# The output projection of the cross attention in three passes of rounded and remaining parts

## What is computed

```
x = x + xattn(layernorm(x), ctx_2048, mask)   # 16 heads of 16 over 257 context rows
x = x + attn(layernorm(x))                    # causal, ternary weights
x = x + ffn(layernorm(x))                     # quantized, 704 wide
```

```
out  = einsum('bhlm,bmhd->blhd', softmax(...), v).reshape(B, L, 256)
out  = out @ wo.T                             # the output projection
gate = sigmoid(rmsnorm(x) @ wg.T)
return gate * out
```

## Time and profile before

| what | us |
|---|---|
| median of 3 runs | 576.29 |
| lowest, highest | 575.0, 815.79 |
| the profiled execution | 573.81 |
| its span (first to last instruction) | 572.0 |

### The profile page before, as it was taken

How to read it: one execution, slowest core, us unless ns; L and a number is a source line. 1 busy time by engine, 2 the same in 40 slices (tenths; PEclk the granted TensorE clock), 3 DMA queues, 4 the chain that set the end, 5 groups by cost and what they waited for, 6 DMA issues and landing times. The chain is left out here.

```text
span 572.0 us, 20510 instructions
## 1 busy us (share of the span) xinstructions
PE 537.9 (94%) x7142; PEld 449.1 (79%) x7142; DVE 445.7 (78%) x1389; ACT 425.1 (74%) x1208; POOL 323.4 (57%) x490
## 2 busy tenths in 40 slices
PE   7898999999999999999999999999999999987785
PEld 6687788788887888888888878888888877865564
DVE  2667585888978787888979787878879776889664
ACT  5987898697878878787977787787878777773221
POOL 5241848566565748566555658475665648372610
PEclk9999999999999999999999999999999999999988
DMA  8532503214233231413142332414142404000000
GB/s 253 182 94 100 144 21 101 58 49 102 59 84 81 71 83 37 126 32 90 54 107 59 77 78 46 117 33 107 39 103 58 105 5 113 21 13 21 24 9 10
DMA packets 42805, 42.34 MB, mean 74 GB/s; under 512 B 16080, under 2 KB 33488, under 8 KB 42704
## 3 DMA queue, kind: packets, MB, share of 16 engines
q1 hardware_dynamic: 42704, 41.03, 27.3%
HBM read 38.26 MB, written 2.75 MB: 72 GB/s over the span
## 5 line engine op out<-in xcount | busy, mean ns | idle before, releaser
L874 ACT ACTIVATE pr<-sm,nb 128x257 f32<-128x257 f32 x256 | 129.2, 508 | 9.4 <-DVE nb L1110 8.0
L662 POOL TENSOR_TENSOR cTl<-cx,cTh 128x516 fp32r<-128x516 f32 x64 | 84.3, 1317 | 75.1 <-ACT cTh L771 75.0
L1110 DVE CUSTOM_DVE_ANT_0 sm<-x_ps,mbias 128x257 f32<-128x257 f32 x256 | 99.3, 419 | 21.9 <-PE x_ps L1416 20.2
L771 ACT ACTIVATE pt<-x_ps 128x512 f32<-128x512 f32 x112 | 65.3, 599 | 10.5 <-PE x_ps L1426 6.9
L1426 PE MATMUL x_ps<-tab,pr 128*128 128x128 f32 x512 | 71.4, 274 | 0.8 <-DVE o L1141 0.4
L771 ACT ACTIVATE kk<-x_ps 128x257 f32<-128x257 f32 x128 | 49.5, 389 | 22.1 <-PE x_ps L1308 22.1
L1426 PEld LDWEIGHTS x_ps<-tab,pr 128*128 128x128 f32 x512 | 57.3, 141 | 5.8 <-issue 4.4
L1308 PE MATMUL x_ps<-cTh,wkTh 128*128 128x258 f32 x256 | 59.7, 315 | 0.4 <-ACT pt L771 0.3
L670 POOL TENSOR_TENSOR sr<-sv,halfneg 128x20 f32<-128x20 f32 x16 | 56.7, 3541 | 1.3
L1308 PE MATMUL x_ps<-wvTh,cTh 128*128 128x256 f32 x256 | 56.8, 303 | 0.0
L1308 PE MATMUL x_ps<-cTl,wkTh 128*128 128x258 f32 x256 | 51.4, 282 | 0.6 <-POOL cTl L662 0.6
(11 more groups left out here) (193 smaller groups left out, 1342.7 us busy)
## 6 DMA issues: line engine op xcount, KB each, us to landing
cx<-in_ctx SPq DMA_DIRECT2D x64, 258.0 KB, 3.9
mbias<-mask_bias SPq DMA_DIRECT2D x64, 128.5 KB, 3.4
xq<-in_x SPq DMA_DIRECT2D x16, 128.0 KB, 2.9
xr<-in_x SPq DMA_DIRECT2D x16, 128.0 KB, 2.8
vx<-end_values SPq DMA_DIRECT2D x64, 32.0 KB, 2.3
vr<-self_values SPq DMA_DIRECT2D x64, 32.0 KB, 1.9
out<-yo SPq DMA_DIRECT2D x16, 128.0 KB, 2.6
fraw<-in_L_ffn_w SPq DMA_DIRECT2D x2, 704.0 KB, 5.2
```

The costliest lines, as they stand in the source:

```text
L662: g.tensor_tensor(cxbuf(cT[1], b)[:, :, :], cx[:, b % BT, :, :], cxbuf(cT[0], b)[:, :, :].bitcast(F32), ALU.subtract).then_inc(A_ctl, 1)
L771: return sc.activation(dst, src, ACT.Copy)
L874: sc.activation(pr[:, b % 2, gr, :], sm[:, b % 2, gr, :], ACT.Exp, bias=nb[:, n:n + 1], scale=-1.0, accum_out=st[:, 0, b, gr:gr + 1]).then ...
L1110: v.tensor_tensor_reduce(out=sm[:, b % 2, gr, :], in0=xb(f"S{b}", gr)[:, 0:LK], in1=mbias[:, b, :], scale=1.0, scalar=0.1 * NEG, op0=ALU.a ...
```

## The change

oTs becomes two fp32r tiles, the rounded part, which ScalarE copies as before, and the remainder, which VectorE takes in a new step B_oT. woT gets two fp32r copies, woS[0] and woS[1]: ScalarE rounds it once in its step WG in tile 0, and GpSimd subtracts once in a new step WO. B_wo on TensorE is then six fp32r matmuls in the place of two fp32 ones. Bank 4 is released after B_oT by the remainder's semaphore, B_oTl, where it was by the copy's, B_oTs. VectorE's new step stands behind B_fin in tile 1, behind D_mx in tile 2, between S(1,1) and S(1,2) in tiles 3 to 13, behind S(1,2) in tile 14, behind D_S in tile 15, and behind C_z(0) in tile 16. The orders of TensorE and ScalarE stay. The counts of SPARE in the tail go from 167 matmuls to 258.

```diff
         "each": [
-            ("D_kT",), ("B_o1",), ("B_O",), ("B_fin",), ("D_S",), ("S", 1, 0), ("S", 1, 1), ("S", 1, 2),
+            ("D_kT",), ("B_o1",), ("B_O",), ("B_fin",), ("D_S",), ("S", 1, 0), ("S", 1, 1), ("B_oT",), ("S", 1, 2),
...
 SPARE = {
-    (16, "B_xT", 0): 20, (16, "B_qkv", 0): 5, (16, "D_PV", 0): 4, (16, "D_yT", 0): 2, (16, "C_hT", 0): 6,
-    (17, "C_xT", 0): 32, (17, "D_PV", 0): 28, (17, "D_yT", 0): 2, (17, "D_pj", 0): 1,
-    (18, "C_xT", 0): 32, (18, "C_z", 0): 3, (18, "C_hT", 0): 28, (18, "C_y", 0): 4,
+    (16, "C_z", 0): 1, (16, "D_kT", 0): 1, (16, "B_wo", 0): 2, (16, "B_xT", 0): 16, (16, "B_qkv", 0): 11,
+    (16, "D_PV", 0): 15, (16, "D_yT", 0): 5, (16, "C_hT", 0): 13, (16, "C_y", 0): 4, (17, "C_xT", 0): 37,
+    (17, "D_kT", 0): 2, (17, "D_S", 0): 4, (17, "D_PV", 0): 44, (17, "D_yT", 0): 5, (17, "C_hT", 0): 3,
+    (17, "D_pj", 0): 2, (17, "C_y", 0): 1, (18, "C_xT", 0): 37, (18, "C_z", 0): 5, (18, "C_hT", 0): 42,
+    (18, "C_y", 0): 8,
 }
...
-        oTs = sb("oTs", [P, 2, P])
+        oTs = [sb("oTsh", [P, 2, P], F32R), sb("oTsl", [P, 2, P], F32R)]
+        woS = [sb("woSh", [P, 2, D], F32R), sb("woSl", [P, 2, D], F32R)]
...
-            ... "B_oT": (B_oTs, 1, -1, 1), ...
+            ... "B_oT": (B_oTl, 1, -1, 1), ...
...
+                    elif k == "WO":
+                        pool.wait_ge(W_wo, 1)
+                        g.tensor_tensor(woS[1][:, :, :], woT[:, :, :], woS[0][:, :, :].bitcast(F32), ALU.subtract).then_inc(W_wo, 1)
...
+                        copy(woS[0][:, :, :], woT[:, :, :]).then_inc(W_wo, 1)
...
+                    elif k == "B_oT":
+                        dve.wait_ge(B_oTs, i)
+                        if due(i - 1):
+                            dve.wait_ge(B_wp, i - 1)
+                        low(oTs[1][:, :, :], xb("B_oT")[:, 0:D].rearrange("p (k c) -> p k c", k=2), oTs[0][:, :, :]
+                            ).then_inc(B_oTl, 1)
...
-                        for m in range(2):
-                            last = mm(xb("B_wo")[:, 0:D], oTs[:, m, :], woT[:, m, :], start=(m == 0), stop=(m == 1))
+                        n = 0
+                        for op, wp in ((0, 0), (0, 1), (1, 0)):
+                            if op:
+                                pe.wait_ge(B_oTl, i)
+                            for m in range(2):
+                                last = mm(xb("B_wo")[:, 0:D], oTs[op][:, m, :], woS[wp][:, m, :], start=(n == 0), stop=(n == 5))
+                                n += 1
```

More of the change, by code:

```diff
@@ L205 @@
             (1, "S", 0, 1), (1, "S", 0, 2), (1, "S", 0, 3), (1, "Q_stats"), (1, "B_den"), (1, "Q_norm"),
[5 rows of a table removed]
-            (2, "B_comb"), (2, "B_den"), (2, "B_o1"), (2, "B_comb2"), (2, "S", 0, 3), (2, "D_kT"), (2, "B_O"),
-            (2, "Q_stats"), (2, "S", 1, 0), (2, "B_fin"), (2, "S", 1, 1), (2, "D_S"), (2, "D_mx"), (2, "Q_norm"),
[3 rows of a table removed]
-            (2, "D_yT"), (2, "D_pj"), (2, "D_xstats"), (2, "D_xq", 0), (2, "D_xq", 1), (2, "D_xq", 2),
+            (1, "B_o1"), (1, "B_comb"), (1, "B_comb2"), (1, "B_O"), (1, "B_fin"), (1, "B_oT"), (1, "S", 1, 0),
[4 rows of a table added]
+            (2, "D_scale"), (2, "B_comb"), (2, "B_den"), (2, "B_o1"), (2, "B_comb2"), (2, "S", 0, 3), (2, "D_kT"),
+            (2, "B_O"), (2, "Q_stats"), (2, "S", 1, 0), (2, "B_fin"), (2, "S", 1, 1), (2, "D_S"), (2, "D_mx"),
[3 rows of a table added]
+            (2, "PT", 2, 1), (2, "D_yT"), (2, "D_pj"), (2, "D_xstats"), (2, "D_xq", 0), (2, "D_xq", 1),
+            (2, "D_xq", 2),
         ],
@@ L229 @@
             (14, "D_scale"), (14, "B_den"), (14, "B_o1"), (14, "B_O"), (14, "Q_stats"), (14, "B_fin"), (14, "D_kT"),
[L230 to L253, removed]
@@ L254 @@
-            (17, "D_xq", 0), (17, "D_xq", 1), (17, "D_xq", 2), (18, "C_z", 0), (18, "C_h", 0), (18, "C_z", 1),
-            (18, "C_h", 1), (18, "C_z", 2), (18, "C_h", 2), (18, "C_q", 0), (18, "C_q", 1), (18, "C_q", 2),
-            (18, "C_y"),
+            (14, "D_S"), (14, "S", 1, 0), (14, "S", 1, 1), (14, "S", 1, 2), (14, "B_oT"), (14, "S", 1, 3),
+            (14, "D_mx"), (14, "B_wo"), (14, "B_x1"), (14, "S", 2, 0), (14, "S", 2, 1), (14, "D_s3"),
+            (14, "S", 2, 2), (14, "B_norm"), (14, "S", 2, 3), (14, "B_xT"), (14, "D_dn"), (14, "C_z", 0),
@@ new lines @@
+            (15, "B_comb"), (15, "B_comb2"), (15, "B_o1"), (15, "D_kT"), (15, "B_O"), (15, "S", 1, 0),
+            (15, "S", 1, 1), (15, "B_fin"), (15, "D_S"), (15, "B_oT"), (15, "S", 1, 2), (15, "D_mx"), (15, "D_s3"),
+            (15, "S", 1, 3), (15, "B_wo"), (15, "D_dn"), (15, "B_x1"), (15, "S", 2, 0), (15, "S", 2, 1),
+            (15, "S", 2, 2), (15, "B_norm"), (15, "S", 2, 3), (15, "B_xT"), (15, "C_z", 0), (15, "C_h", 0),
+            (15, "D_p3"), (15, "D_p4"), (15, "B_qkv"), (15, "S", 3, 0), (15, "S", 3, 1), (15, "C_z", 1),
@@ new lines @@
+            (15, "C_h", 1), (15, "C_z", 2), (15, "C_h", 2), (15, "C_q", 0), (15, "C_q", 1), (15, "C_q", 2),
+            (15, "D_yT"), (15, "S", 3, 2), (15, "S", 3, 3), (15, "PT", 2, 1), (15, "C_y"), (15, "D_pj"),
+            (15, "D_xstats"), (16, "B_den"), (15, "D_xq", 0), (15, "D_xq", 1), (16, "B_comb"), (15, "D_xq", 2),
+            (16, "B_comb2"), (16, "B_o1"), (16, "B_O"), (16, "B_fin"), (16, "D_scale"), (16, "C_z", 0),
+            (16, "B_oT"), (16, "D_kT"), (16, "C_h", 0), (16, "C_z", 1), (16, "B_wo"), (16, "C_h", 1), (16, "B_x1"),
@@ new lines @@
+            (16, "D_S"), (16, "C_z", 2), (16, "B_norm"), (16, "D_mx"), (16, "D_s3"), (16, "B_xT"), (16, "C_h", 2),
+            (16, "D_dn"), (16, "D_p3"), (16, "D_p4"), (16, "C_q", 0), (16, "C_q", 1), (16, "B_qkv"), (16, "C_q", 2),
+            (16, "D_yT"), (16, "C_y"), (16, "D_pj"), (16, "D_xstats"), (16, "D_xq", 0), (16, "D_xq", 1),
+            (16, "D_xq", 2), (17, "D_scale"), (17, "D_kT"), (17, "C_z", 0), (17, "C_h", 0), (17, "D_S"),
+            (17, "D_mx"), (17, "C_z", 1), (17, "D_s3"), (17, "C_h", 1), (17, "C_z", 2), (17, "D_dn"),
@@ L514, in perceiver @@
         RELEASE = {
-            "B_st": (B_o1, 1, -1, 1), "B_O": (B_o2, 1, -1, 1), "B_oT": (B_oTs, 1, -1, 1), "B_wo": (B_u1, 1, -1, 1),
+            "B_st": (B_o1, 1, -1, 1), "B_O": (B_o2, 1, -1, 1), "B_oT": (B_oTl, 1, -1, 1), "B_wo": (B_u1, 1, -1, 1),
             "B_xT": (B_xTl, 1, -1, 1), "B_qkv": (B_sq, 1, -1, 1), "D_QT": (B_qTs, 1, -2, 1), "D_kT": (B_kbd, 1, -2, 1),
@@ L894, in body @@
                             act.wait_ge(B_wp, i - 1)
[L895 removed]
+                        copy(oTs[0][:, :, :], xb("B_oT")[:, 0:D].rearrange("p (k c) -> p k c", k=2)).then_inc(B_oTs, 1)
                     elif k == "B_keep":
```

23 lines of the change are left out of this document (16 added, 7 removed), and 21 rows, old and new, of the table SCHEDULE.

## The result

| | before | after |
|---|---|---|
| median, us | 574.75 | 577.08 |
| lowest, us | 573.18 | 575.84 |
| the profiled execution, us | 573.81 | 576.39 |
| its span, us | 572.0 | 574.6 |

Both medians are of ten runs. The ratio is 1.004, with an interval of 1.0029 to 1.0051; it leaves out one disturbed run of before (815.79 us). The change makes the kernel 0.4% slower. The forecast was 581, with +4.9 us against the +2.3 measured (+2.6 between the profiled executions). The sign was right and the size was twice too large. Of the 3.9 us between 581 and 577.08, 1.5 is not the change's: the forecast was put on the median of the three runs shown, 576.3, and that of ten is 574.75.

The account below looks back on a forecast made before the run. VectorE's list was taken to bound each period from D_S to B_xT, TensorE's the rest. The terms 3.4 + 1.0 + 0.3 + 1.1 + 0.15 - 1.1 = +4.9 us on 576.3 gave 581 us, range 572 to 586.

Parts of the forecast that it names:

- What bounds the kernel: Each period: VectorE's list sets the pace from D_S to B_xT with 0.08 us slack, TensorE's list the rest.
- B_wo on TensorE: Output projection: six fp32r matmuls hold TensorE 0.71 us instead of 0.95, saving 0.24 a tile (lower bound 0.14).
- The wait for the remainder: Before B_wo: remainder ready at 206.11, TensorE wants it at 206.50; costs nothing in tiles 3 to 13.
- VectorE's new step: Tiles 3 to 13: step costs 0.39 us, xn comes 0.31 later each tile, +3.4 us (bounds 2.9 and 4.3).
- The wait before B_xT: TensorE's wait for xn before its transpose would be 0.85 us a tile, swallowing what the projection saved.
- Tile 1: The new step waits for ScalarE's copy before S(1,0) and delays what follows, +1.0 us (bounds 0.3 and 1.1).
- The weight's split and tile 2: Weight copy and subtraction in tile 0 fall into idle time; in tile 2 VectorE waits anyway: 0 each.
- Tiles 14 to 16: The new step's delays there: +0.3 us in tile 14, +1.1 in tile 15, +0.15 in tile 16.
- The tail: Added SPARE matmuls lift the granted clock behind the wait before 549.25, -1.1 us (gain between 0 and 1.7).
- that rival: The tail's added matmuls don't fit their gaps, up to 10.9 us on the path, up to 592 us; chance 0.05.
- GpSimd's rival: The new step is held up by a GpSimd operation of 1.97 us, about 602 us; chance 0.04.
- the first rival: TensorE's saving comes through, each tile 0.24 us shorter, tail gain 1.1, 572 us; chance 0.25.

Follow-up runs that it names:

- the kernel with two passes: The kernel after without VectorE's step and without the third matmul pass, bank released by ScalarE's copy: 571.38 us (0.9941), period 31.48.
- the two experiments: The kernel after with the old SPARE counts: 578.30 us (1.0054); the kernel before with the new SPARE counts: 573.03 us (0.9969).

## Why the prediction was half right

**What bounds the kernel.** Right. The period has a part that VectorE's list sets, and TensorE's saving in B_wo vanished in it. The kernel with fp32 matmuls and the step kept has the same period. That TensorE's list sets the other part fits its 22.6 us, which stay whatever was done in the first, but no experiment took work off TensorE there.

**B_wo on TensorE.** Mis-sized, with no effect: 0.80 us, not 0.71. It is near the lower bound, by the 0.08 us of leaving for the scores' matmuls, which the forecast put on entering instead.

**The wait for the remainder.** Right in tiles 3 to 13: the step ends at 207.42, TensorE wants it at 207.84.

**VectorE's new step, +0.31 us a tile, +3.4 us over the eleven tiles.** This is the term that failed: it measured +1.0 us. The mechanism was the forecast one, and the size was wrong in three ways. The step holds VectorE for 0.35 us and not 0.39: it starts 0.02 us behind the end of ScalarE's copy, and no wait of 0.05 comes on top of the hold. The slack was 0.18 us and not 0.08: I took D_s3 to hold VectorE for its length of 0.69, though I had read S by its starts (0.35 behind an S of 0.42). From start to start D_s3 holds it for 0.59 in after (0.63 in the kernel with two passes, where it starts 0.15 us before GpSimd's D_vbd ends, as in before). Together that is +0.17 us in the place of +0.31, and 1.9 us over 11 tiles in the place of 3.4. The periods of after, 31.81 or 31.82 in eight of eleven tiles, bear it out.

Third, D_S moved apart by only 1.95 - 0.98 = 0.97 us over those tiles, and not by 1.9. The rest lies in uneven periods. From D_S to D_S, before has 31.90, 32.07, 31.76 and 31.91 us in tiles 7, 8, 9 and 12, together 1.0 us more than at the usual 31.66; after has 32.16 in tile 9 and 31.71 in tile 5, together 0.25 us more than at 31.81. So 1.9 - 1.0 + 0.25 = 1.1, near the 0.97. In tiles 7 and 12 of before and in tile 9 of after the delay (0.33 to 0.35 us) begins with a stop of VectorE; the one in tile 7 of before, and then the one in after:

```profile
242.47 0.43 DVE L1110 CUSTOM_DVE_ANT_0 sm<-x_ps,mbias 128x257 f32<-128x257 f32 x1 [0.32 <-issue]
```

```profile
304.96 0.69 DVE L1232 TENSOR_TENSOR soft<-soft,mx 128x512 f32<-128x512 f32 x1 [0.25 <-issue]
```

VectorE waits there for nothing that the profile shows. In tile 8 of before no such stop shows: there most of the 0.4 us comes up behind B_xT, where GpSimd is idle for 0.3 us longer in front of L740, again with no releaser. The long periods follow the program and not chance. They come in tiles 7, 8 and 12 of before and of the two kernels made from it by new counts and by Q_stats moved, and in tiles 7 and 12 of the kernel with two passes, which has VectorE's steady list of before. They come once, in tile 9, in after and in the three made from it that keep its steady order, and nowhere in the three made from after with Q_stats before D_S. What they are was not settled.

Here 0.42 us of length hold VectorE for 0.35, and 0.67 for 0.59. The rule that the prediction cited from the Trainium skill ("VectorE: DVE Perf Modes", "The DRAIN you can't avoid"), that the next operation does not start until the pipe is empty, does not hold for these steps, and would have made the term larger still; the same section adds that an operation which is not held starts earlier, and with that the trace agrees.

**The wait before B_xT.** I expected 0.8 us of it in each tile. It stayed as it was, because TensorE's wait moved: V(2) needs a bank that VectorE's S(2,1) reads, and waits there. V(2) starts 0.52 us behind the last pair of C_z(0) (210.60 - 210.08), where before has 0.20, and the 0.32 us between them is what B_wo saved (0.15) and what VectorE's list grew by (0.17). The groups by line of after, against the 4.1 us of the earlier trace rows:

```profile
L1517 PE MATMUL x_ps<-tab,xn 128*128 128x128 f32 x32 | 6.9, 296 | 3.4 <-DVE xn L1193 1.8 <-DVE nb L1118 1.5
...
L1509 PE MATMUL x_ps<-woSh,oTsh 128*128 128x256 f32 x32 | 6.7, 290 | 0.8 <-DVE oTsl L977 0.7
```

The chain from VectorE to TensorE has more than one link, and the first of them takes the wait.

**Tile 1, +1.0.** Right, to 0.04 us and by the rows that were named. The timeline of after:

```profile
48.12 0.42 DVE L977 TENSOR_TENSOR oTsl<-x_ps,oTsh 128x256 fp32r<-128x256 f32 x1 [0.95 <-ACT oTsh L778]
...
48.92 0.52 ACT L882 ACTIVATE pr<-sm,nb 128x257 f32<-128x257 f32 x1 [0.83 <-DVE nb L1118]
...
51.59 0.69 PE L1430 MATMUL x_ps<-kk,qbd 32*64 32x257 f32 x16 [1.18 <-ACT kk L778]
```

The subtraction starts at the forecast 48.12, the exponential at 48.92 (forecast 48.93), and S(2) 0.96 us later than before.

**The weight's split and tile 2, 0.** Right: B_wo of tile 1 starts 0.03 us later in after, and tile 2 adds 0.02 (0.96 to 0.98).

**Tiles 14 to 16.** Tile 14 costs +0.23 by the start of tile 15 (forecast 0.3), tile 15 +1.3 (forecast 1.1: 0.45 at B_wo, the rest at PT(1,0), which waits for an exponential), tile 16 nothing in the end (forecast 0.15).

**The tail, -1.1.** Near: -0.9 between the two profiles, and -1.2 and -1.8 in the two experiments. The sum is not made as forecast, though: by C_z(2) of tile 18 the tail had given back 1.3 us (3.50 - 2.16), part of it in a second stretch that the forecast did not name (560 to 564, granted clock 0.57 in before and 1.00 in after), and 0.4 of it was lost again by C_hT. The added matmuls cost less than they bring, and that rival is out.

**GpSimd's rival** is out: the step took 0.42 us beside an operation of 1.97 on GpSimd. Q_norm, whose tensors both lie in SBUF, fared otherwise: 1.47 us in place of 0.41. The Trainium skill ("SBUF — State Buffer", "Who interferes with whom") says that VectorE contends with GpSimd when it has two SBUF inputs, or in the two-port mode that a `tensor_scalar` can enter, and not otherwise. The runs agree in four cases: the step, the division, Q_norm, and D_s3, which has two SBUF inputs and took 1.12 us in place of 0.67. The forecast looked at GpSimd for the new step alone and not for the D_s3 behind it.

**The ranges.** 577.08 lies in the forecast's 572 to 586, but just under the 578 that the bounds of my terms allowed. The bound of 2.9 us for the eleven tiles had the hold of the step at 0.34 and the same mistaken slack; a bound that does not vary the slack is no bound. That the measured time is in the range at all is owed to the first rival, whose 572 had drawn the range down.

## What to carry to other kernels

Before a step is inserted, find which engine's list sets each part of a period and how much slack it has, and read every hold from start to start, not from lengths: an error of 0.1 us in the slack was worth 1.1 us over the eleven tiles. Place the new step where its producer has surely ended, and where nothing that another engine soon needs stands behind it. Two unlucky places cost twice as much as eleven steady tiles, and one step moved into an idle slot, with the tail's gain, turned the loss into a gain, while three steps moved without asking who was behind them cost 4.5 to 5%.
